# Score products in another order, and one output split moved on VectorE, in a fused attention and expert kernel

## The chip, the cores and the metric

One core of a Trainium2 chip runs the whole program. Its engines work side by side and meet at semaphores: TensorE (PE; its weight loads are listed apart as PEld), VectorE (DVE), ScalarE (ACT), GpSimd (POOL), and SyncE (SP), which issues most transfers. The metric is device time in microseconds (us) of one execution.

## The reference

Everything is float32. x is 32 batches of 256 tokens of width 256, ctx has the same shape, and no key is masked by the input mask.

```
y = x + xattn(layernorm(x), ctx, ctx, Wq, Wk, Wv, Wo, bo, mask)     # 16 heads of 64, causal
out = y + ffn(layernorm(y))

xattn: q = qn@Wq, k = ctx@Wk, v = ctx@Wv          # 256 -> 1024
       dots = q k^T / 8, masked and causal; attn = softmax(dots); (attn v) @ Wo + bo
ffn:   expert = argmax(y_n @ router_w.T + router_b)   # 32 experts
       relu(relu(y_n @ w1[e] + b1[e]) @ w2[e] + b2[e])  for the token's own expert
```

## The kernel before

There are two phases. The first does attention and routing for the 32 batches, one after the other, and writes each token's normalised row into a list of its expert in HBM. The second goes through these lists. The change touches the first phase alone, which takes all but about the last 215 us.

Each engine has its own stream of instructions, written out by hand. A batch b has four **steps**, s = 0 to 3. A step deals with a **quad** of four heads, which are two pairs: i = 0 and i = 1. The two heads of a pair are its two **sides**, and they lie in the two halves of the partitions, so that their two products of 64 rows run on TensorE at the same time. In a step TensorE does, in this order (`iteration` of the tensor block):

- `scores(*ahead, 0, ...)`: the products of queries and keys of pair 0 of the *next* quad, into two banks of psS. Since attention is causal, query rows 0 to 127 need 128 keys (a **narrow** product, 128 columns, it = 0), rows 128 to 255 need 256 (a **wide** one, it = 1). Between narrow and wide stands the wait list `first_ready`.
- `probs_t(b, s, 0)`: the first 4 of the 12 blocks of this quad's probabilities are transposed into psR, by 8 products of 64 columns (line 629).
- `scores(*ahead, 1, ...)`: the same for pair 1, with the wait list `second_ready` between narrow and wide. This is "the second half of a step's scores".
- `probs_t(b, s, 1)`: the other 8 blocks, 16 products.
- `values`: attention output of the quad before, into psO (line 650).
- **pieces**: projections and small products named in `PIECES` ("v1", "q0", "wo", "x2" and so on; "wo" is the product with Wo of the batch before, in step 0), each into one of the three banks of psR.

Float32 products are done in two passes. So the narrow part of a pair is four matrix instructions in the trace (two sides, two passes), and so is the wide part; each has a weight load of its own.

`second_ready` is what `probs_t(b, s, 1)` needs before it writes into psR: the probabilities are normalised (s_pn), the transposes of part 0 have ended (s_pt_half, counted up by the last of them), and the bank 2 of psR was read by whoever reads the last piece in it. In step 1 that is `residual` on VectorE (s_x1, line 943), which reads "wo".

```
def second_ready(b, s, prev, nxt):
    pe.wait_ge(s_pn, 4 * G(b, s))
    pe.wait_ge(s_pt_half, G(b, s))
    for bank, (name, at) in last_in(b, s, prev, nxt).items():
        if bank == 2:
            pe.wait_ge(*emptied(name, at))
```

ScalarE copies psR into PT (line 792), takes the exponentials (`exps`, line 799), and writes the high part of the attention output, OT_hi (`hi_o`, line 807). VectorE masks the scores as they leave psS (`masked`, line 1097, eight instructions a step), multiplies by the reciprocal of the sums (`normalised`, lines 1103 to 1112), writes the low part of the output, OT_lo (`lo_o`, line 1117), and routes tokens in a chain of small instructions (`largest`, `where_largest`, `expert_ids`, `one_hot`, `counted` and so on). `mask_of` (lines 1075 and 1079) makes the mask of the next batch, which the masking of step 3 reads. `lo_o` counts s_o up. TensorE's `values` waits for the s_o of the quad whose output lay in psO before, and "wo" waits for that of its batch's last quad.

Of the kernel before, what the change touches and what calls it, by code (L numbers as in the profile page):

```python
# [16 lines left out]
P = 128  # L17
# [12 lines left out]
def attention_moe(nc, x, ctx, mask, Wq, Wk, Wv, Wo, bo, router_w, router_b, w1, b1, w2, b2, out):  # L30
# [21 lines left out]
    with ExitStack() as es:  # L52
# [190 lines left out]
        def pieces(s, prev, nxt):  # L243

            if s == 0 and not prev:
                return FIRST_0
            return [(name, off) for name, off in PIECES[s] if (off >= 0 or prev) and (off <= 0 or nxt)]
# [5 lines left out]
        def bank_of(s, name, prev, nxt):  # L253
            names = [n for n, off in pieces(s, prev, nxt)]
            return banks(len(names))[names.index(name)]
# [37 lines left out]
        def G(b, s):  # L293

            return QUADS * b + s + 1

        def later(b, s, nxt):

            if s < QUADS:
                return b, s  # L300
            return (b + 1, s - QUADS) if nxt else None
# [199 lines left out]
        def _(pe):  # L501
# [74 lines left out]

            def scores(b, s, i, between=None):
                p = 2 * s + i
                for it, o in ((0, 0), (1, P)):
                    if it and between:  # L580
                        between()
                    for side in range(2):
                        rows = slice(DH * side, DH * side + DH)
                        last = nc.tensor.matmul(psS[:, 2 * i + side, o:o + (it + 1) * P], QT[rows, p, it * P:(it + 1) * P],  # L584
                                                KT[rows, p, 0:(it + 1) * P], start=True, stop=True)
                last.then_inc(s_sc, 1)
# [181 lines left out]
        def dve_read(name, b, bank):  # L768

            src = psR[:, bank, :]  # L770
            if name[0] == "v":
                i = int(name[1])
                nc.vector.wait_ge(s_v_pe, 4 * b + i + 1)
                nc.vector.tensor_copy(V[:, i % 2, 512 * (i // 2):512 * (i // 2) + 512], src[:, :]).then_inc(s_v, 1)  # L774
            elif name == "xt":
                nc.vector.wait_ge(s_xt_hi, b + 1)
                nc.vector.tensor_tensor(flat(XTl), src[:, :], flat(XTh), ALU.subtract).then_inc(s_xt, 1)  # L777
            elif name == "lg":

                nc.vector.wait_ge(s_lg_pe, b + 1)  # L780
                for it in range(TT):
                    last = nc.vector.tensor_tensor(lg[:, it, :], src[:, it * E:(it + 1) * E], rb_b[:], ALU.add)
                last.then_inc(s_lg, 1)
# [128 lines left out]
        def _(dve):  # L912
# [178 lines left out]
            def masked(b, s, i, side):  # L1091

                if side == 0:
                    wait_apart(dve, s_passed, s_sc, 2 * G(b, s) - 1 + i)
                for it, o in ((0, 0), (1, P)):
                    cols, k = slice(o, o + (it + 1) * P), 4 * i + 2 * side + it
                    nc.vector.tensor_tensor_reduce(out=Sm[:, 2 * (s % 2) + i, side, cols], in0=psS[:, 2 * i + side, cols],  # L1097
                                                   in1=MK[:, cols], scale=-SCALE, scalar=3e38, op0=ALU.add, op1=ALU.min,
                                                   accum_out=mneg[:, s % 2, k:k + 1]).then_inc(s_sm, 1)
# [15 lines left out]
            def lo_o(b, s):  # L1115
                dve.wait_ge(s_o_hi, G(b, s))
                nc.vector.tensor_tensor(OTl[:, 2 * s:2 * s + 2, :].rearrange("p a n -> p (a n)"), psO[:, :],  # L1117
                                        OTh[:, 2 * s:2 * s + 2, :].rearrange("p a n -> p (a n)"), ALU.subtract).then_inc(s_o, 1)
# [7 lines left out]
            def iteration(b, prev, prev2, nxt, more):  # L1126
                for s in range(QUADS):
                    ahead = later(b, s + 1, nxt)
                    here = pieces(s, prev, nxt)

                    def read(*names):
                        for name, off in here:
                            if name in names:
                                dve_read(name, b + off, bank_of(s, name, prev, nxt))

                    def mask(i, side):
                        if ahead:
                            masked(*ahead, i, side)

                    def norm(i):  # L1140
                        if ahead:
                            normalised(*ahead, i)

                    def route(on, at, stage):
                        if on:
                            stage(at)

                    if s == 0:
                        mask(0, 0)
                        route(prev2, b - 2, rows_gap)  # L1150
                        mask(0, 1)
                        route(prev2, b - 2, rows_near)
                        mask(1, 0)
                        route(prev2, b - 2, rows_all)
                        mask(1, 1)
                        route(prev2, b - 2, rows_kept)
                        if nxt:
                            sum_ctx(b + 1)
                        route(prev2, b - 2, row_places)
                        if prev:  # L1160
                            lo_o(b - 1, QUADS - 1)
                        route(prev2, b - 2, row_numbers)
                        if more and prev:
                            stats1(b + 2)
                        norm(0)
                        if prev:
                            read("xt")
                        norm(1)
                        route(prev2, b - 2, fills)
                        if not prev:  # L1170
                            read("xt")
                            lo_wo(0)
                            stats1(b + 2)
                        elif more:
                            apply1(b + 2)
                        if nxt:
                            first_key(b + 1)
                    if s == 1:
                        if prev:
                            residual(b - 1, bank_of(0, "wo", prev, nxt))  # L1180
                        mask(0, 0)
                        mask(0, 1)
                        mask(1, 0)
                        mask(1, 1)
                        if prev:
                            stats2(b - 1)
                        norm(0)
                        read("v3")
                        norm(1)
                        lo_o(b, 0)  # L1190
                        if prev:
                            apply2(b - 1)
                        else:
                            lo_wo(1)
                            apply1(b + 2)
                    if s == 2:
                        mask(0, 0)
                        mask(0, 1)
                        mask(1, 0)
                        mask(1, 1)  # L1200
                        norm(0)
                        read("lg")
                        route(prev, b - 1, largest)
                        read("v0")
                        norm(1)
                        route(prev, b - 1, where_largest)
                        if nxt:
                            mask_of(b + 1)
                        route(prev, b - 1, expert_ids)
                        route(prev, b - 1, one_hot)  # L1210
                        lo_o(b, 1)
                    if s == 3:
                        if nxt:
                            halve_of(b + 1)
                        mask(0, 0)
                        mask(0, 1)
                        mask(1, 0)
                        mask(1, 1)
                        norm(0)
                        read("v1")  # L1220
                        route(prev, b - 1, counted)
                        route(prev, b - 1, tiles_over)
                        route(prev, b - 1, tiles_more)
                        norm(1)
                        route(prev, b - 1, tiles_run)
                        route(prev, b - 1, tiles_next)
                        route(prev, b - 1, rows_next)
                        lo_o(b, 2)
# [29 lines left out]
            with dve.Fori(2, B - 2) as b:  # L1258
                iteration(b, True, True, True, True)
# [297 lines left out]
```

## Time and profile before

| | us |
|---|---|
| median of 3 runs | 1508.87 |
| lowest, highest | 1504.34, 1510.36 |
| the profiled execution, whole | 1513.0 |
| its span, from the first to the last instruction | 1511.3 |

The profile's page has the span's busy times by engine, the share of busy time in 40 slices, the chain that ended last, and the costliest groups. The trace was asked further for the order in time of a few stretches of one batch in the middle of the first phase. A batch repeats every 41.2 us there.

### The profile page before, as it was taken

What the parts mean: (1) busy time and instruction counts of PE and PEld (TensorE: products, weight loads), DVE (VectorE), ACT (ScalarE), POOL (GpSimd) and SP (SyncE); (2) the same over time, 40 slices, a digit from 0 to 9 for tenths busy, and PEclk for the clock granted to TensorE, in tenths of its full rate; (3) what the DMA queues carried; (4) which work ended last, traced back from release to release, by engine and by line L of the source; (5) the groups of instructions that cost most, each with busy time, mean ns of one, the idle gap of its engine ahead of it and who ended that gap; (6) DMA issues with size and microseconds to landing.
All of it is one profiled execution on the core that took longest, in us unless ns stands there. A gap on an engine that the chain in (4) does not pass through costs nothing.

```text
span 1511.3 us, 43956 instructions
## 1 busy us (share of the span) xinstructions
PE 1479.1 (98%) x14165; PEld 1283.4 (85%) x14165; DVE 1231.7 (82%) x5088; ACT 1013.6 (67%) x3144; POOL 360.6 (24%) x507
## 2 busy tenths in 40 slices
PE   8999999999999999999999999999999999978997
PEld 7898888888888888888888888888888888865775
DVE  5888888988888888888988888888888988755663
ACT  5767667667677667677666677677677677633663
POOL 3112212211121122222211121122222211112777
PEclk9999999999999999999999999999999999987998
DMA  8643000000000000000000000010000000005650
GB/s 288 128 150 115 29 21 29 29 22 29 29 22 25 25 29 29 27 23 29 29 22 29 28 23 22 29 29 29 23 27 29 29 22 22 15 8 175 212 174 12
DMA packets 70410, 77.85 MB, mean 52 GB/s; under 512 B 11351, under 2 KB 64221, under 8 KB 70369
## 3 DMA queue, kind: packets, MB, share of 16 engines
q1 hardware_dynamic: 62546, 60.37, 13.8%
q0 software_dynamic: 7680, 16.93, 3.1%
q8 instruction: 22, 0.36, 0.1%
q14 instruction: 18, 0.15, 0.0%
q10 hardware_dynamic: 144, 0.03, 0.0%
HBM read 47.61 MB, written 33.88 MB: 54 GB/s over the span
## 4 chain that ended last, share of the span: by engine, by line
PE 93%; DVE 3%; ACT 1%; DMA 1%; POOL 1%; issue 1%; SPq 0%; POOLq 0%; DVEq 0%
PE psR L514 37%; PE psS L584 14%; PE psO L650 12%; PE psR L546 12%; PE psR L629 6%; PE psS L1496 4%; PE psR L505 2%; PE psR L1486 2%; PE psR L556 2%; PE psR L1483 1%; PE psR L1473 1%; PE psO L1473 1%; DVE Sm L1112 0%; ACT Sm L799 0%; DMA lists<-stg,lrow 0%
## 5 line engine op out<-in xcount | busy, mean ns | idle before, releaser
L799 ACT ACTIVATE Sm<-Sm,mneg 128x128 f32<-128x128 f32 (+1 forms) x1024 | 453.5, 456 | 153.6 <-DVE mneg L1097 153.6
L1097 DVE CUSTOM_DVE_ANT_0 Sm<-psS,MK 128x128 f32<-128x128 f32 (+1 forms) x1024 | 303.7, 353 | 4.4 <-PE psS L584 1.9
L792 ACT ACTIVATE PT<-psR 128x512 f32<-128x512 f32 x384 | 201.6, 598 | 134.8 <-PE psR L629 130.9
L584 PE MATMUL psS<-KT,QT 64*128 64x128 f32 (+1 forms) x2048 | 251.5, 356 | 5.0 <-DVE V L774 2.0
L799 ACT ACTIVATION_READ_ACCUMULATOR Sm<-Sm,mneg 128x1 f32 x1024 | 205.5, 201 | 0.0
L650 PE MATMUL psO<-PT,V 128*64 128x256 f32 (+1 forms) x2048 | 196.0, 334 | 0.6 <-DVE OT_lo L1117 0.3
L1112 DVE SCALAR_TENSOR_TENSOR Sm<-Sm,halve,rinv 128x512 f32<-128x512 f32 x256 | 191.4, 748 | 0.0
L584 PEld LDWEIGHTS psS<-KT,QT 64*128 64x128 f32 x2048 | 148.7, 187 | 30.4 <-issue 7.7
L650 PEld LDWEIGHTS psO<-PT,V 128*64 128x64 f32 x2048 | 127.4, 137 | 49.0 <-DVE OT_lo L1117 1.2
L629 PEld LDWEIGHTS psR<-ident,Sm 64*128 64x128 f32 x3072 | 144.5, 139 | 21.1 <-DVE Sm L1112 2.5
L1103 DVE RECIPROCAL rinv<-rsum 128x4 f32<-128x4 f32 x256 | 44.1, 172 | 135.6 <-ACT Sm L799 132.3
L629 PE MATMUL psR<-ident,Sm 64*128 64x64 f32 x3072 | 140.9, 223 | 2.2 <-DVE Sm L1112 2.2
L1109 DVE SCALAR_TENSOR_TENSOR Sm<-Sm,halve,rinv 128x256 f32<-128x256 f32 x256 | 124.1, 485 | 9.1
L756 ACT ACTIVATE KT<-psR 128x512 f32<-128x512 f32 x128 | 75.6, 591 | 55.0 <-PE psR L514 55.0
L514 PE MATMUL psR<-CT_hi,Wk_hi 128*128 128x256 f32 x512 | 108.0, 293 | 1.3 <-ACT PT L792 1.3
L1329 POOL DMA_INDIRECT out<-Y,tok x96 | 94.0, 979 | 49.4 <-issue 27.4
L514 PE MATMUL psR<-XT_hi,Wq_hi 128*128 128x256 f32 x512 | 103.5, 284 | 2.0 <-DVE XT_lo L777 1.3
L514 PE MATMUL psR<-XT_lo,Wq_hi 128*128 128x256 f32 x512 | 103.3, 283 | 0.0
L756 ACT ACTIVATE QT<-psR 128x512 f32<-128x512 f32 x128 | 76.5, 598 | 39.8 <-PE psR L514 39.7
L514 PE MATMUL psR<-CT_lo,Wk_hi 128*128 128x256 f32 x512 | 103.0, 283 | 0.0
L514 PE MATMUL psR<-XT_hi,Wq_lo 128*128 128x256 f32 x512 | 103.0, 283 | 0.0
L514 PE MATMUL psR<-CT_hi,Wk_lo 128*128 128x256 f32 x512 | 102.7, 282 | 0.0
(155 smaller groups left out, 3061.7 us busy)
## 6 DMA issues: line engine op xcount, KB each, us to landing
lists<-pad SPq DMA_DIRECT2D x8, 1560.0 KB, 10.2
XS<-lists SPq DMA_DIRECT2D x48, 260.0 KB, 2.9
x_in<-in_x SPq DMA_DIRECT2D x32, 256.0 KB, 3.0
ctx_in<-in_ctx SPq DMA_DIRECT2D x32, 256.0 KB, 2.6
xr<-in_x SPq DMA_DIRECT2D x32, 256.0 KB, 2.6
W2R<-in_L_ffn_weights SPq DMA_DIRECT2D x1, 2048.0 KB
out<-Y,tok POOLq DMA_INDIRECT x96, 2.4
W2R<-in_L_xattn_Wv SPq DMA_DIRECT2D x2, 512.0 KB, 9.3
```

Of the source, the lines that this page charges most:

```text
L514: last = nc.tensor.matmul(dst, a(k), z(k), start=(n == 0), stop=(n == 3 * len(ks) - 1))
L546: last = nc.tensor.matmul(dst[:, it * D:(it + 1) * D], a[:, t, rows], z[:, t, :], start=(it == 0 and a is OTh and z is Woh and t == 0), st ...
L584: last = nc.tensor.matmul(psS[:, 2 * i + side, o:o + (it + 1) * P], QT[rows, p, it * P:(it + 1) * P], KT[rows, p, 0:(it + 1) * P], start=T ...
L629: last = nc.tensor.transpose(ring[:, o:o + DH], Sm[rows, 2 * (s % 2) + i, side, src:src + P], ident[rows, rows])
L650: last = nc.tensor.matmul(psO[DH * side:DH * side + DH, i * N + t * P:(i + 1) * N], V[:, t, DH * h:DH * h + DH], blocks_of[:, blocks, :, : ...
L756: nc.scalar.activation(T[:, 2 * c:2 * c + 2, :].rearrange("p a n -> p (a n)"), src[:, :], ACT.Copy).then_inc(done, 1)
L792: nc.scalar.activation(PT[:, s % 2, 512 * k:512 * k + 512], psR[:, k, :], ACT.Copy).then_inc(s_pt, 1)
L799: nc.scalar.activation(v, v, ACT.Exp, bias=mneg[:, s % 2, k:k + 1], scale=-1.0, accum_out=rsum[:, s % 2, k:k + 1]).then_inc(s_exp, 1)
L1097: nc.vector.tensor_tensor_reduce(out=Sm[:, 2 * (s % 2) + i, side, cols], in0=psS[:, 2 * i + side, cols], in1=MK[:, cols], scale=-SCALE, sc ...
L1109: nc.vector.scalar_tensor_tensor(out=v, in0=v, scalar=halve[:, 0:1], in1=of[:, :, 0:1].broadcast_to([P, 2, P]), op0=ALU.mult, op1=ALU.mult ...
L1112: nc.vector.scalar_tensor_tensor(out=v, in0=v, scalar=halve[:, 1:2], in1=of[:, :, 1:2].broadcast_to([P, 2, N]), op0=ALU.mult, op1=ALU.mult ...
L1329: nc.gpsimd.indirect_dma_start(out_rows, bass.IndirectOffsetOnAxis(ap=tok[u][:, t:t + 1], axis=0), Y[u][:, t, :], None, bounds_check=last_ ...
```

## The change

In `scores`, the pair i = 1 now does its wide product first and its narrow one second; the waits stay between the two. Pair 0 is as it was. In VectorE's step 2, `lo_o(b, 1)`, which stood last, comes right after `where_largest`; `expert_ids` comes next, and the mask of the next batch after it.

```diff
             def scores(b, s, i, between=None):
                 p = 2 * s + i
-                for it, o in ((0, 0), (1, P)):
-                    if it and between:
+                for n, (it, o) in enumerate((((0, 0), (1, P)), ((1, P), (0, 0)))[i]):
+                    if n and between:
                         between()
...
                         norm(1)
                         route(prev, b - 1, where_largest)
+                        lo_o(b, 1)
+                        route(prev, b - 1, expert_ids)
                         if nxt:
                             mask_of(b + 1)
-                        route(prev, b - 1, expert_ids)
                         route(prev, b - 1, one_hot)
-                        lo_o(b, 1)
```

TensorE's order in step 2 of the loop's batch, second half of the scores (psS takes the scores, KT and QT are keys and queries; L619 belongs to `second_ready`); - is before, + is now:

```order
 L584 MATMUL psS<-KT,QT 128x256
 L629 MATMUL psR<-ident,Sm 128x64 x8
-L584 MATMUL psS<-KT,QT 128x128 x2
+L584 MATMUL psS<-KT,QT 128x256 x2
 L619 REGISTER_ALU [waits first_pair_probsT_in_psum,probs_normalised]
-L584 MATMUL psS<-KT,QT 128x256 [waits q_ready]
-L584 MATMUL psS<-KT,QT 128x256
+L584 MATMUL psS<-KT,QT 128x128 [waits q_ready]
+L584 MATMUL psS<-KT,QT 128x128
 L629 MATMUL psR<-ident,Sm 128x64 x16
 L650 MATMUL psO<-PT,V 64x256 [waits probsT_ready,out_ready]
```

What stood behind the waits and stands ahead of them now is the two products of 256 columns; the two of 128 are behind. The other steps read the same, with other names in the wait.

VectorE's order at the end of step 2 of the loop's batch (OT_lo is the output split, MK the mask, eid and OH the routing, halve the first thing of step 3):

```order
 L973 MAX_INDEX ix<-mx,lg 128x8 [waits route_chain]
 L973 MAX_INDEX ix<-mx,lg 128x8
+L1117 TENSOR_TENSOR OT_lo<-psO,OT_hi 128x512 [waits out_hi]
+L977 REGISTER_ALU
+L978 CAST eid<-ix 128x2 [waits route_chain]
 L1075 SCALAR_TENSOR_TENSOR MK<-maskrow,causal 128x256
 L1079 SCALAR_TENSOR_TENSOR MK<-maskrow,causal 128x128
-L977 REGISTER_ALU
-L978 CAST eid<-ix 128x2 [waits route_chain]
 L981 REGISTER_ALU
 L982 TENSOR_TENSOR OH<-iota_e,eid 128x64 [waits route_chain]
-L1117 TENSOR_TENSOR OT_lo<-psO,OT_hi 128x512 [waits out_hi]
 L1086 TENSOR_SCALAR dead_half<-iota_p,firstk 128x2 [waits mask_chain]
```

The output split passed four instructions, and the cast passed two. The streams of ScalarE, GpSimd and SyncE are the same.

## Rows read from the trace of the kernel before

**Rows 1.** The page: span, and busy time by engine

```profile
span 1511.3 us, 43956 instructions
PE 1479.1 (98%) x14165; PEld 1283.4 (85%) x14165; DVE 1231.7 (82%) x5088; ACT 1013.6 (67%) x3144; POOL 360.6 (24%) x507
```

**Rows 2.** Timeline, step 2: start us, us, engine, line, operation, count, [idle before <-releaser]

```profile
710.85 0.48 PEld L629 LDWEIGHTS psR<-ident,Sm 64*128 64x128 f32 x8
...
711.07 0.41 PE L629 MATMUL psR<-ident,Sm 64*128 64x64 f32 x8
711.25 0.31 PEld L584 LDWEIGHTS psS<-KT,QT 64*128 64x128 f32 x4
711.31 1.11 PE L584 MATMUL psS<-KT,QT 64*128 64x128 f32 x8
...
711.72 0.31 PEld L584 LDWEIGHTS psS<-KT,QT 64*128 64x128 f32 x4 [0.16 <-issue]
...
712.04 0.74 PEld L629 LDWEIGHTS psR<-ident,Sm 64*128 64x128 f32 x16
...
712.25 0.66 PE L629 MATMUL psR<-ident,Sm 64*128 64x64 f32 x16
...
712.85 1.28 PEld L650 LDWEIGHTS psO<-PT,V 128*64 128x64 f32 x16
```

**Rows 3.** Timeline, second half of the scores in step 1

```profile
701.00 0.69 DVE L943 TENSOR_TENSOR stg<-psR,xr 128x512 f32<-128x512 f32 x1
...
701.49 1.06 PE L584 MATMUL psS<-KT,QT 64*128 64x128 f32 x8
...
702.35 0.69 PE L629 MATMUL psR<-ident,Sm 64*128 64x64 f32 x16
```

**Rows 4.** Timeline of TensorE, step 3: second half of the scores

```profile
721.04 0.98 PE L584 MATMUL psS<-KT,QT 64*128 64x128 f32 x8
721.83 0.69 PE L629 MATMUL psR<-ident,Sm 64*128 64x64 f32 x16
```

**Rows 5.** Timeline of weight loads, the same stretch

```profile
722.52 0.20 PEld L650 LDWEIGHTS psO<-PT,V 128*64 128x64 f32 x4 [0.15 <-DVE OT_lo L1117]
```

**Rows 6.** Timeline of TensorE, step 0: second half of the scores

```profile
689.84 0.97 PE L584 MATMUL psS<-KT,QT 64*128 64x128 f32 x8
690.62 0.69 PE L629 MATMUL psR<-ident,Sm 64*128 64x64 f32 x16
```

**Rows 7.** Timeline of VectorE, end of step 2 and start of step 3

```profile
720.92 0.41 DVE L1075 SCALAR_TENSOR_TENSOR MK<-maskrow,causal 128x256 bf16<-128x256 uint8 x1
...
721.45 0.16 DVE L978 CAST eid<-ix 128x2 f32<-128x2 uint32 x1
...
721.79 0.68 DVE L1117 TENSOR_TENSOR OT_lo<-psO,OT_hi 128x512 fp32r<-128x512 f32 x1
722.39 0.22 DVE L1086 TENSOR_SCALAR dead_half<-iota_p,firstk 128x2 f32<-128x2 f32 x1
```

**Rows 8.** Timeline of VectorE: first normalising of step 3, a batch apart; step 0's split

```profile
684.64 0.18 DVE L1103 RECIPROCAL rinv<-rsum 128x4 f32<-128x4 f32 x1 [0.69 <-ACT Sm L799]
...
693.69 0.68 DVE L1117 TENSOR_TENSOR OT_lo<-psO,OT_hi 128x512 fp32r<-128x512 f32 x1
...
725.89 0.18 DVE L1103 RECIPROCAL rinv<-rsum 128x4 f32<-128x4 f32 x1 [0.69 <-ACT Sm L799]
```

**Rows 9.** Timeline of ScalarE in step 3: PT copies

```profile
722.55 1.57 ACT L792 ACTIVATE PT<-psR 128x512 f32<-128x512 f32 x3 [1.80 <-PE psR L629]
```

**Rows 10.** Busy time by stretch: us, then PE, PEld, DVE, ACT, POOL (instructions), clock, DMA

```profile
684.64:694.38 9.74, 9.74 (x100) 8.61 (x99) 9.57 (x48) 6.84 (x21) 0.43 (x2) 1.00 0.00 0
```

**Rows 11.** Timeline of weight loads, start of "wo" in step 0

```profile
694.53 0.78 PEld L546 LDWEIGHTS psR<-Wo_hi,OT_hi 128*128 128x128 f32 x6
```

**Rows 12.** Who waited for whom, 683.9 to 725.15 us (one batch)

```profile
POOL first_masked L392 <- DMA maskrow<-in_mask_BxS_bf: 25.9, 2, 13.0
...
DVE xn L932 <- POOL rstd L387: 0.3, 1, 0.3
```

## The prediction

> **What bounds the kernel now.** The page comes first [rows 1]: TensorE is busy for 1479 of 1511 us, VectorE for 1232, ScalarE for 1014. So TensorE bounds the kernel, but "busy" reaches from a product's start to its modelled end, and short idle times hide under it. So the second view is the timeline of single steps, read by starts.
>
> In step 2 [rows 2] the last of the first 8 transposes ends at 711.48 (711.07 + 0.41). The second half of the scores starts at 711.31. Its first weights are loaded from 711.25. The load of the wide product's weights starts only at 711.72, 0.24 us after the transposes ended, and the row calls 0.16 us of idle time "issue". That is the wait for the transposes' own semaphore, and the instructions behind it. From 711.72 on all runs without a gap: the last wide pass starts at 712.04 (the loads for the transposes go ahead under it) and the transposes at 712.25. So a wide pass takes 0.21, and the load ahead of the first one 0.32 - 0.21 = 0.11. A narrow pass has half the columns: 0.11. The narrow product, with a load of 0.11 from 711.25 and two passes, ends at about 711.58. The array is idle from there to 711.83 (711.72 + 0.11): 0.25 us.
>
> From the first narrow start to the first transpose it takes 0.94 in step 2, 0.86 in step 1 [rows 3], 0.79 in step 3 [rows 4] and 0.78 in step 0 [rows 6]. Without a wait it would be 0.05 (rest of the first load) + 2 x 0.21 + 2 x 0.11 = 0.69. The excess is the idle time: 0.25, 0.17, 0.09 and 0.09.
>
> Third, what TensorE gets from the others. In step 1 the wait list holds VectorE's `residual`, which ends at 701.69 [rows 3], 0.20 after the half started at 701.49. The transposes' semaphore must come at about the same place, since in step 2 they end 0.17 after the half's start. So step 1 is a near tie of TensorE's own transposes and VectorE's chain. In step 0 "wo" starts its loads at 694.53 [rows 11], and the output split that it waits for ends at 694.37 [rows 8]. A wait took 0.24 from end to load in step 2, so this too is nearly a tie. In step 3 the values load at 722.52, with 0.15 of idle time put down to the split [rows 5], which ends at 722.47 [rows 7].
>
> **The change part by part.**
>
> *Wide first, steps 0 and 3.* The wait now stands behind two wide passes, which end 0.05 + 0.43 = 0.48 after the half's start. The restart of the old order comes earlier: the transposes end 0.17 after the start, and the narrow end (0.27) plus an idle time of 0.09 is 0.36. So the wait is wholly covered and the half takes 0.69: a gain of 0.09 in each.
>
> *Step 2.* The restart stays where it is, since the transposes set it: load at 0.41, first pass at 0.52, 0.04 past the end of the wide passes. What is left is two narrow passes, not two wide ones: 0.73 in place of 0.94, a gain of 0.21.
>
> *Step 1.* If `residual` keeps its distance, the restart is at 0.27 + 0.17 = 0.44, covered by 0.48: a gain of 0.17. If TensorE comes earlier against it, the gain within the half rises to 0.21 at most, but the lead is lost to the wait.
>
> TensorE's own sum is 0.09 + 0.17 + 0.21 + 0.09 = 0.56 a batch.
>
> *The output split.* It moves ahead of the mask and the cast, from 721.79 to about 720.92 [rows 7], 0.87 earlier, so that it ends at about 721.60, far ahead of the values. In step 3 it takes 0.69 from the start of the 16 transposes (721.83) to the values' load (722.52) [rows 4, 5]; in step 2, 0.60 (712.25 to 712.85) [rows 2]. So 0.09 us a batch goes. What ScalarE must have done for the split (OT_hi) is not new: it reads the step's values, which ended in the step's first third, and nothing shows an idle time of VectorE there. Behind the split now stand the cast, the mask and the one-hot rows. The mask comes about 0.7 later, ahead of the masking as before, since the work up to line 1086 (722.39) is the same. The mask's semaphore also lets SyncE load the next mask row, 0.7 later; GpSimd waits for that load up to 13.0 us and then for others [rows 12], so it is hidden, until it is 13 us late. The cast and the one-hot instruction no longer stand right behind what they wait for: up to 0.1 us less, in front of ScalarE's exponentials. For these VectorE waits 0.69 anyway [rows 8], so it is counted as nothing.
>
> TensorE alone would then gain 0.56 + 0.09 = 0.65 a batch. **What is late next** decides how much of it stays. VectorE's first normalising in step 3 waits for ScalarE [rows 8], ScalarE's copies wait for the transposes [rows 9], so this point moves with TensorE: 0.09 from its start of step 3. From there VectorE is busy for 9.57 of 9.74 us, up to the split of step 0 [rows 10]; it then goes on to `residual`, behind a norm that GpSimd holds up by 0.3 [rows 12]. This chain gains no more than its anchor's 0.09. TensorE arrives at "wo" 0.09 (step 3) + 0.09 (split) + 0.09 (step 0) = 0.27 earlier, finds the split only 0.09 earlier, and has a margin of 0.16 less the latency of a wait, which I take as 0.04 (bounds: 0, if a wait costs 0.16 from end to load; 0.10, if 0.06). So 0.13 stays at "wo". Then comes step 1's half with its 0.17, or 0.21 if `residual` is late: together 0.30 for these three steps (bounds 0.26 and 0.30), and so most of the part that belongs to the split is lost to this tie. Step 2 adds its 0.21. The chain in step 2 has cover: VectorE waits for ScalarE there for up to microseconds, and both for TensorE.
>
> **The sum.** 0.21 + 0.30 = 0.51 us a batch, over 31 batches with four such halves: 15.8 us. The profiled execution took 1513.0, of which 1511.3 is the span; it would take 1497.2. It lies 4.1 over the median of 1508.87, on which I put the gain, about a hundredth: **1493**.
>
> **The rivals.**
>
> *The chain of VectorE leaves TensorE's gain alone* (faster still). If the waits of "wo" and `residual` have 0.15 us of margin more than I read, all 0.65 stays: 20 us, 1489. For it speaks that the trace names no waiting of TensorE at these two places; against it, how near the two ends lie [rows 3, 8, 11]. Chance 0.2.
>
> *VectorE's chain does not move with TensorE* (no difference). If something other than the transposes sets ScalarE's or VectorE's pace in steps 2 and 3, the tie in step 1 gives back what was gained before it, and 0.17 to 0.21 of one half is left: 5 to 6.5 us, about 1503. Against it: VectorE idles for 0.69 and ScalarE for 1.80 in each step 3 [rows 8, 9]. Chance 0.13.
>
> *The narrow weights are not loaded under the wide passes* (slower). In the old order no scores' load followed a wide pass within the half. If each narrow load waited until the passes ahead were through, the half would take 0.48 + 2 x (0.11 + 0.11) = 0.92 against 0.94, 0.86, 0.79 and 0.78: 0.31 more a batch, less nothing else, 10 us or 1519; it decides from a load exposed by more than 0.14 us a half on average, where the 0.56 is used up. Against it: the transposes' loads start at 710.85 under a wide pass, whose successors start at 711.07, 0.22 later, a pass and no more [rows 2]. Chance 0.06.
> The Trainium skill says in "TensorE: Matmul & The Clock Gate", Part 3 (Packing small matmuls, The mechanism), that a weight load overlaps running products only where its row group differs. By that rule this rival would be the forecast, with a time of 1519. The trace disagrees, since loads for both halves of the rows go ahead under passes on both.
>
> *The change does half of what it says*, because the sequencer needs the covered time for its wait instructions anyway, and the restart slips by 0.1 to 0.2 in each half: a gain of about 0.25 a batch, 8 us, 1501. Chance 0.08.
>
> **How the numbers follow.** The forecast has 0.53. "Same" is within 0.5% of 1508.87, or 7.5 us, about what a measurement of this kernel can tell from no change. Faster: 0.53 + 0.2 + half of the last rival, 0.77. Same: 0.13 + 0.04 = 0.17. Slower: 0.06. The range reaches from 1487 (the faster rival, with 2 us of scatter between runs) to 1503; the slower rival and the far half of the second lie outside.
>
> **What the profile would show.** TensorE in step 2: from the half's first start to the first of the 16 transposes 0.73, in the others 0.69 to 0.81. Step 3: values load 0.60 behind the transposes' start, and no idle time put down to OT_lo. Step 0: "wo" starts its load close behind the end of the split, with an idle time ahead of it. Step 1: the restart follows `residual`. A batch takes 40.7 us, not 41.2 [rows 8]. The forecast is wrong if halves take 0.9 (loads exposed), or if they take 0.7 and the batch is still 41.0 or more (the chain took the gain).

## The result, and the profile after

| | before | changed |
|---|---|---|
| median, us (4 runs each) | 1507.11 | 1489.49 |
| lowest, highest | 1504.34, 1510.36 | 1485.65, 1491.09 |
| ratio, with its 95% interval | | 0.9865 [0.9837, 0.9893] |
| the profiled execution, whole | 1513.0 | 1485.65 |
| its span | 1511.3 | 1483.9 |
| one batch, from the traces | 41.26 | 40.65 |

By the ratio the changed kernel is 1.35% faster. The two medians lie 17.6 us apart, which is 1.2% and inside the interval. The forecast was 1493, with 15.8 us of gain from 0.51 us a batch; a batch gained 0.61.

The page of the changed kernel answers to [rows 1]:

```profile
span 1483.9 us, 43956 instructions
PE 1453.8 (98%) x14165; PEld 1264.7 (85%) x14165; DVE 1224.8 (83%) x5088; ACT 1011.6 (68%) x3144; POOL 358.3 (24%) x507
```

The two spans lie 27.4 us apart, which is more than the change is worth. Two windows of each kernel show why: the first phase up to where its last scores are, and what is behind (first before, then changed; columns as in [rows 10]: us, PE, PEld, DVE, ACT and POOL with instructions, granted clock, DMA share, GB/s).

```profile
16.00:1328.30 1312.30, 1305.39 (x13018) 1151.18 (x13020) 1122.96 (x4719) 918.44 (x2916) 254.36 (x374) 1.00 0.13 39
1328.30:1511.30 183.00, 161.56 (x1065) 120.41 (x1061) 100.61 (x354) 87.73 (x219) 99.03 (x102) 0.89 0.39 120
```

```profile
16.00:1310.00 1294.00, 1287.15 (x13022) 1137.05 (x13023) 1115.38 (x4718) 916.73 (x2916) 252.70 (x374) 1.00 0.14 40
1310.00:1484.00 174.00, 154.05 (x1065) 115.43 (x1061) 101.33 (x354) 87.50 (x219) 98.86 (x102) 0.94 0.41 126
```

The first phase gives 18.3 us (31 batches at 0.61 are 18.9). The other 9 us of the spans lie in the second phase, which has the same 1065 products in both and a mean granted clock of 0.89 against 0.94 (where it falls is shown in the last section). The change does not touch that phase. In the experiments it also varies more than the change is worth, so steps are compared below by the first phase alone, whose clock is 1.00 everywhere.

**Batch by batch.** `residual` (line 943) runs once a batch. Its instructions between 600 and 800 us, first and last start, before and changed; four batches lie between the two:

```profile
L943 DVE TENSOR_TENSOR stg<-psR,xr x5: 692/692/692, 618.5 to 783.5; 128x512 f32<-128x512 f32 x5
```

```profile
L943 DVE TENSOR_TENSOR stg<-psR,xr x5: 692/692/692, 610.6 to 773.2; 128x512 f32<-128x512 f32 x5
```

165.0 / 4 is 41.25, and 162.6 / 4 is 40.65.

**The second half of the scores, step 2**, timeline of TensorE and of its weight loads in the changed kernel, which answers to [rows 2]:

```profile
701.82 0.41 PE L629 MATMUL psR<-ident,Sm 64*128 64x64 f32 x8
702.07 0.91 PE L584 MATMUL psS<-KT,QT 64*128 64x256 f32 x8
702.80 0.66 PE L629 MATMUL psR<-ident,Sm 64*128 64x64 f32 x16
```

```profile
702.01 0.31 PEld L584 LDWEIGHTS psS<-KT,QT 64*128 64x128 f32 x4
702.47 0.31 PEld L584 LDWEIGHTS psS<-KT,QT 64*128 64x128 f32 x4 [0.16 <-issue]
702.69 0.63 PEld L629 LDWEIGHTS psR<-ident,Sm 64*128 64x128 f32 x16
```

The wait is still there, with the same 0.16 us of idle time ahead of the second four loads. The transposes end at 702.23 (701.82 + 0.41), and the load starts 0.24 later, as before. But now two wide passes, until 702.55 (0.48 behind the half's start, as the prediction worked it out), run beside it. From the half's first start to the 16 transposes it takes 0.73 (702.80 - 702.07), where it took 0.94.

The other three, step 3, 0 and 1, which answer to [rows 4], [rows 6] and [rows 3], read 0.71 each (671.65 - 670.94 and so on):

```profile
670.94 0.87 PE L584 MATMUL psS<-KT,QT 64*128 64x256 f32 x8
671.65 0.66 PE L629 MATMUL psR<-ident,Sm 64*128 64x64 f32 x16
```

```profile
680.81 0.87 PE L584 MATMUL psS<-KT,QT 64*128 64x256 f32 x8
681.52 0.66 PE L629 MATMUL psR<-ident,Sm 64*128 64x64 f32 x16
```

```profile
692.42 0.87 PE L584 MATMUL psS<-KT,QT 64*128 64x256 f32 x8
693.13 0.66 PE L629 MATMUL psR<-ident,Sm 64*128 64x64 f32 x16
```

The step that ends with a given half, by the distance from one second half to the next in the traces' own resolution (us). Most tables below are of this kind; step 0's number holds what happens from step 0's half to that of step 1, with "wo" in it.

| from the half of | before | changed | gain |
|---|---|---|---|
| step 3 to step 0 | 10.048 | 9.867 | 0.181 |
| step 0 to step 1 | 11.647 | 11.617 | 0.030 |
| step 1 to step 2 | 9.833 | 9.647 | 0.186 |
| step 2 to step 3 | 9.733 | 9.520 | 0.213 |
| a batch | 41.26 | 40.65 | 0.61 |

**The values of step 3** answer to [rows 5]: the load comes 0.58 behind the transposes (672.23 - 671.65), not 0.69, and no idle time stands ahead of it. The split that it waits for ran at 670.82, ahead of the cast and the mask, where it stood behind them [rows 7]:

```profile
672.23 0.85 PEld L650 LDWEIGHTS psO<-PT,V 128*64 128x64 f32 x12
```

```profile
670.82 0.67 DVE L1117 TENSOR_TENSOR OT_lo<-psO,OT_hi 128x512 fp32r<-128x512 f32 x1
671.41 0.16 DVE L978 CAST eid<-ix 128x2 f32<-128x2 uint32 x1
671.47 0.42 DVE L1075 SCALAR_TENSOR_TENSOR MK<-maskrow,causal 128x256 bf16<-128x256 uint8 x1
```

**"wo" in step 0**, weight loads, which answers to [rows 11], and the split that it waits for, which answers to [rows 8]:

```profile
684.83 0.58 PEld L505 LDWEIGHTS psR<-ident,xn 128*128 128x128 f32 x4
685.48 0.65 PEld L546 LDWEIGHTS psR<-Wo_hi,OT_hi 128*128 128x128 f32 x5
```

```profile
684.68 0.68 DVE L1117 TENSOR_TENSOR OT_lo<-psO,OT_hi 128x512 fp32r<-128x512 f32 x1
```

The small piece ahead of "wo" (line 505) starts its loads 0.65 before those of "wo". Before, these were 0.56 apart (693.97 and 694.53), and so they are in an experiment below that takes this wait away, so 0.56 is how the loads run without a wait. So TensorE now waits here for 0.09, and starts 0.12 behind the end of the split (685.36). This idle time is too short to carry a name in the rows.

### The profile page after: what moved, and what is told of

It reads as the page before. It is cut to its first block, busy times and chain, and to the rows that moved or that the text cites. A ratio compares the mean times of both kernels' runs of the same rounds, so it can differ in the third digit from the quotient of the medians.

```text
span 1483.9 us, 43956 instructions
## 1 busy us (share of the span) xinstructions
PE 1453.8 (98%) x14165; PEld 1264.7 (85%) x14165; DVE 1224.8 (83%) x5088; ACT 1011.6 (68%) x3144; POOL 358.3 (24%) x507
## 4 chain that ended last, share of the span: by engine, by line
PE 93%; DVE 3%; ACT 1%; POOL 1%; issue 1%; DMA 1%; ACTq 0%; DVEq 0%; SPq 0%; POOLq 0%
PE psR L514 37%; PE psS L584 13%; PE psR L546 13%; PE psO L650 12%; PE psR L629 6%; PE psS L1496 3%; PE psR L505 2%; PE psR L1486 2%; PE psR L556 2%; PE psR L1483 1%; PE psR L1473 1%; PE psO L1473 1%; DVE Sm L1112 0%; ACT Sm L799 0%; POOL out L1329 0%
## 5 line engine op out<-in xcount | busy, mean ns | idle before, releaser
L584 PE MATMUL psS<-KT,QT 64*128 64x256 f32 (+1 forms) x2048 | 232.9, 345 | 4.8 <-DVE V L774 2.2
L584 PEld LDWEIGHTS psS<-KT,QT 64*128 64x128 f32 x2048 | 153.4, 187 | 34.0 <-issue 7.2
L629 PEld LDWEIGHTS psR<-ident,Sm 64*128 64x128 f32 x3072 | 134.2, 139 | 14.6 <-DVE Sm L1112 2.7
L629 PE MATMUL psR<-ident,Sm 64*128 64x64 f32 x3072 | 137.8, 222 | 2.4 <-DVE Sm L1112 2.4
L392 POOL CAST first_masked<-maskrow 128x1 f32<-128x1 uint8 x32 | 6.2, 194 | 418.3 <-DMA maskrow<-in_mask_BxS_bf 418.3
```

The costliest lines, as they stand in the source:

```text
L629: last = nc.tensor.transpose(ring[:, o:o + DH], Sm[rows, 2 * (s % 2) + i, side, src:src + P], ident[rows, rows])
```

## The experiments

Every kernel is compared with the kernel before on the same chip. The first four ran on one whose second phase takes some 30 us longer (the kernel before takes 1544.06 there, 13 runs); in the first phase the steps that an edit does not touch agree with the first profiles' to 0.01 us.

### The scores' order alone

```diff
-                for it, o in ((0, 0), (1, P)):
-                    if it and between:
+                for n, (it, o) in enumerate((((0, 0), (1, P)), ((1, P), (0, 0)))[i]):
+                    if n and between:
```

> The order of the scores as changed, the output split left at the end of step 2. Theory A (read from the two traces): in the second halves TensorE gains 0.07, 0.15, 0.21 and 0.07 us in steps 0 to 3 (first start to first transpose), and 0.03 more in steps 0, 1 and 3 at the last transpose. In step 3 the values wait for the output split, which stays 1.43 us after the half's start, so that step gives back its 0.10. A batch takes 40.75 to 40.8 us (before 41.26, changed 40.65): ratio about 0.989 to 0.990. Theory B (the prediction on record): most of what the split gives is lost at wo anyway, so this is as fast as the whole change within 0.05 us a batch, 40.65 to 40.7.

1529.58 against 1544.06: 0.9911 [0.9889, 0.9932]. A batch takes 40.82, a gain of 0.45 of the change's 0.61. Theory A had 40.75 to 40.8 and is close; theory B, with at most 40.7, is refuted. The steps from 3, 0, 1, 2 take 10.049, 11.598, 9.647 and 9.522. The halves are those of the changed kernel. But step 3 gained nothing: what its half saves is given back at its values. Timeline, TensorE and the loads:

```profile
670.96 0.87 PE L584 MATMUL psS<-KT,QT 64*128 64x256 f32 x8
671.67 0.65 PE L629 MATMUL psR<-ident,Sm 64*128 64x64 f32 x16
```

```profile
672.44 0.63 PEld L650 LDWEIGHTS psO<-PT,V 128*64 128x64 f32 x8 [0.25 <-DVE OT_lo L1117]
```

The idle time ahead of the values was 0.15 with the old order [rows 5] and is 0.25 here, with the split as releaser, which in this kernel starts at 671.71 as the last of step 2's instructions. The gain of 0.10 in step 3's half and the growth of this wait by 0.10 cancel.

### The output split alone

```diff
+                        lo_o(b, 1)
+                        route(prev, b - 1, expert_ids)
                         if nxt:
                             mask_of(b + 1)
-                        route(prev, b - 1, expert_ids)
                         route(prev, b - 1, one_hot)
-                        lo_o(b, 1)
```

> The output split moved as changed, the scores in the old order. Theory A: values in step 3 load 0.08 us earlier, but at wo in step 0 TensorE meets VectorE's split with a margin of about 0.05, so a batch gains 0.05: 41.21 us, ratio 0.998 to 1.000. Theory B (parts add up): the whole change's 0.61 less what the scores alone give, 0.10 to 0.15 a batch: 41.12 to 41.16, ratio 0.997. Rival (the split pushes the mask and routing back, which costs): over 41.26.

1541.43 against 1544.06: 0.9977 [0.9957, 0.9997]. A batch takes 41.20, a gain of 0.06, as theory A had it (41.21), and not 0.10 or more. Its reason was another, though: the step with "wo" is as long as before (11.647). Only step 3 changes (9.993 for 10.048): at its values 0.08 is won, and 0.025 of it is lost again in the products that follow.

The two parts alone come to 0.45 + 0.06 = 0.51 us a batch; together they bring 0.61. The split is worth 0.06 by itself and 0.165 once the scores have their new order (40.82 to 40.65), since then it must also keep step 3's own 0.10.

### No product ahead of the wait

From the kernel before: the waits of the second half stand ahead of both its products, so that nothing runs while TensorE waits.

```diff
-                    if it and between:
+                    if it != i and between:
```

> From the kernel before: the waits of the second half stand ahead of both its products, narrow and wide, so that nothing covers them. Theory A (the restart is set by the wait, and what stands behind it is added): second halves, from the restart's first product to the first transpose, have load, two narrow and two wide passes behind the wait. From the last of the first 8 transposes the step 2 half takes 0.21 us more than before (two narrow passes leave the cover), and the others as much, so a batch takes about 4 x 0.21 = 0.84 more, less what ties give back: 41.9 to 42.1 us, ratio 1.014 to 1.021. Rival (the sequencer needs the time for the wait instructions anyway, wherever they stand): no more than 0.3 a batch, 41.3 to 41.6.

1567.86 against 1544.06: 1.0159 [1.0132, 1.0187], 0.77 us a batch slower (42.03), inside theory A's 41.9 to 42.1. Each of the four halves, read from the start of the first 8 transposes to that of the 16, is 0.22 longer; of these 0.89 in sum, 0.77 reach the batch, and where the rest is made up was not followed. Timeline of step 2, TensorE and its loads:

```profile
723.91 0.41 PE L629 MATMUL psR<-ident,Sm 64*128 64x64 f32 x8
724.57 0.93 PE L584 MATMUL psS<-KT,QT 64*128 64x128 f32 x8 [0.25 <-PE psR L629]
725.32 0.66 PE L629 MATMUL psR<-ident,Sm 64*128 64x64 f32 x16
```

```profile
724.56 0.53 PEld L584 LDWEIGHTS psS<-KT,QT 64*128 64x128 f32 x8 [0.38 <-issue]
```

Here the idle time is plain to see, and for once it carries the transposes' name. It makes a series of three with one edit, what stands ahead of the wait. From the start of the first 8 transposes to the start of the 16, step 2: nothing ahead 1.41 (725.32 - 723.91), the narrow product ahead 1.18 (712.25 - 711.07, [rows 2]), the wide one ahead 0.98 (702.80 - 701.82). The work is the same in all three. Each step of it hides about 0.2 us more: the narrow product covers its own two passes of 0.11, and the wide one in its place covers two passes of 0.21.

### "wo" waits for the low part only where it reads it

From the changed kernel: "wo" reads the high part of the output first, in its first 16 products, and the low part behind them. The wait for the low part (s_o) now stands there, and the one ahead of all is for the high part alone.

```diff
-                pe.wait_ge(s_o, G(b, pairs[-1] // 2))
+                pe.wait_ge(s_o_hi, G(b, pairs[-1] // 2))
...
                     for a, z in ((OTh, Woh), (OTh, Wol), (OTl, Woh)):
+                        if it == 0 and a is OTl:
+                            pe.wait_ge(s_o, G(b, pairs[-1] // 2))
```

> The changed kernel, with wo waiting for the high part of the output (out_hi) at its start and for the low part only ahead of the products that read it. Theory A (TensorE loses 0.07 us a batch at wo, since the low part comes late): a batch takes 40.58 us, ratio to the kernel before 0.984 to 0.986, and step 0 from its second half to that of step 1 takes 11.55 in place of 11.62. Rival (TensorE loses nothing at wo; the 0.04 us that step 0 is short of its gain lies elsewhere, in the step's copies or transposes): 40.65, no change to the changed kernel.

1520.24 against 1544.06: 0.9847 [0.9826, 0.9867]. A batch takes 40.55, 0.10 less than the changed kernel, and all of it in the step from 0 to 1 (11.520 for 11.617). Theory A had 40.58 and 11.55; the rival's 40.65 is refuted. Weight loads at "wo", and the split on VectorE:

```profile
683.42 0.58 PEld L505 LDWEIGHTS psR<-ident,xn 128*128 128x128 f32 x4
683.98 1.01 PEld L548 LDWEIGHTS psR<-Wo_hi,OT_hi 128*128 128x128 f32 x8
```

```profile
683.27 0.68 DVE L1119 TENSOR_TENSOR OT_lo<-psO,OT_hi 128x512 fp32r<-128x512 f32 x1
```

"wo" is again 0.56 behind the piece ahead of it. From the half of step 3, which starts at 669.54 here, it starts its loads after 14.44; in the changed kernel after 14.54 (685.48 - 670.94), and before after 14.74 (694.53 - 679.79, where 679.79 is the half's start a batch ahead of [rows 4]). So TensorE reaches "wo" 0.30 earlier than it used to, and the changed kernel keeps 0.20 of it.

### The changed kernel, once more, beside its variants

> The changed kernel itself, on the chip and in the rounds of e6, as the reference for it and for the first four. Batches 40.65 us, attention phase 1293.7 us from first to last scores as in its first trace, whatever the chip; ratio to the kernel before 0.986 to 0.989.

On another chip, where the kernel before takes 1512.67 (7 runs): 1487.13, a ratio of 0.9833 [0.9806, 0.9859], and a batch of 40.65, as expected. The ratio lies below the expected 0.986 to 0.989: the medians are 25.5 us apart here and were 17.6 in the first comparison, while the loop is the same. From the first to the last scores it takes 1291.8 us, not 1293.7. The 31 batches account for no more than 0.2 of this difference, so it lies outside the loop, in the phase's two ends.

### With "wo" as above, and `residual`'s wait for it last

`residual` on VectorE waits for "wo" first, and then for the bias and for two scatters that have long ended. Here the wait for "wo" stands behind these.

```diff
-                dve.wait_ge(s_wo_pe, b + 1)
                 dve.wait_ge(s_bo, 2 * b + 2)
                 if not isinstance(b, int) or b > 0:
                     for it in range(TT):
                         wait_apart(dve, s_passed, s_scat[it], 16 * b)
+                dve.wait_ge(s_wo_pe, b + 1)
```

> e4 and, in VectorE's residual of step 1, the wait for wo's product moved behind the three waits that are satisfied long before. Theory A (residual starts 0.43 us after wo's product ended because its other waits are worked off only then, and VectorE is free 0.08 before): residual starts 0.08 to 0.15 us earlier against step 1's second half, and the batch stays at 40.55, since the wide passes cover that wait. Rival (the chain through GpSimd and the norm sets residual, as the prediction had it): it keeps its distance of 0.49 ahead of the second half's start.

1485.59 against 1512.67: 0.9835 [0.9808, 0.9862], not to be told from the changed kernel by its time. A batch takes 40.55, as without this edit. Timeline of VectorE ahead of `residual` (line 945 here), of this kernel and, as the second, of the changed one:

```profile
649.66 0.42 DVE L1073 TENSOR_REDUCE firstk<-mtmp 128x1 f32<-128x256 f16 x1
650.08 0.69 DVE L945 TENSOR_TENSOR stg<-psR,xr 128x512 f32<-128x512 f32 x1
```

```profile
691.43 0.42 DVE L1071 TENSOR_REDUCE firstk<-mtmp 128x1 f32<-128x256 f16 x1
691.94 0.69 DVE L943 TENSOR_TENSOR stg<-psR,xr 128x512 f32<-128x512 f32 x1
```

In this kernel `residual` follows the instruction ahead of it without a gap, as it nearly does before the change (700.57 + 0.42 to 701.00): VectorE's own work holds it, and no order of waits can bring it forward. In the changed kernel it starts 0.09 behind. There it follows TensorE: it starts 0.45 after the end of "wo", which is at 691.49:

```profile
690.37 1.12 PE L546 MATMUL psR<-Wo_hi,OT_lo 128*128 128x256 f32 x8
```

Theory A is wrong: `residual` starts 0.47 ahead of step 1's second half here, and so it does in the kernel without this edit. It took the gap of 0.09 from the changed kernel, but letting "wo" start earlier had already closed it. The rival has the distance right; its cause, the chain through GpSimd, was not tested apart from VectorE's own work.

### The kernel before, with `residual`'s waits in that order

The same edit of `residual` in the kernel before.

> The kernel before with only the waits of residual reordered. Theory A and the prediction's tie agree here that VectorE's own chain ends 0.01 us before residual starts: no change, batch 41.26, second half of step 1 0.86. If the chain has room after all, that half falls to 0.78, as in steps 0 and 3, and the batch to 41.18.

One execution, 1507.92, beside 1512.67; its batch takes 41.26, as before. The half of step 1 shrinks from 0.86 to 0.85 and nothing else comes of it, as expected. So `residual` did not cost the old kernel more than 0.01 a batch, although it lands in the middle of the half.

## Why the prediction was right in its main reading, and the step that failed

The step that failed is the term for "wo" in step 0. The prediction let VectorE's chain gain no more than 0.09 there, so that 0.13 of TensorE's lead was kept; the chain gained 0.16 and 0.20 was kept. That is 0.07 of the 0.10 us by which a batch gained more than forecast. With this term fell the conclusion that most of the split's worth is lost. The rest comes from step 1's half, 0.19 for 0.17, and from rounding.

| us a batch | forecast | measured | |
|---|---|---|---|
| halves of steps 0, 1, 2, 3 | 0.69, 0.69, 0.73, 0.69 | 0.71, 0.71, 0.73, 0.71 | right |
| gained on the path in the halves | 0.56 | about 0.60 | a term left out |
| the split, at the values of step 3 | 0.09 | 0.08 | right |
| TensorE arrives at "wo" earlier by | 0.27 | 0.30 | |
| VectorE's split is done earlier by | 0.09 | 0.16 | the step that failed |
| of TensorE's lead at "wo" is kept | 0.13 | 0.20 | mis-sized by it |
| step 1, to the half of step 2 | 0.17 | 0.19 | |
| step 2, to the half of step 3 | 0.21 | 0.21 | right |
| a batch | 0.51 | 0.61 | |

**The covered wait.** The main reading was right: the restart after the transposes' semaphore costs the same as before, and what changes is what runs beside it. The series of three above shows this as a cause: what stands ahead of the wait was made both less and more, and the time followed.

**A small term was missing.** The halves come out 0.02 longer than forecast, and yet the gain by steps is 0.10, 0.19, 0.21 and 0.10, 0.04 more in sum than the 0.56. The reason is what "the half" is measured to. The two sides of a pair run beside each other in two halves of the rows. After the old wait the wide passes of the two sides restarted 0.036 apart in steps 0 and 3 (single records of the trace: 721.609 and 721.645), so the last transposes ended later than the first one's start says; in the new order the sides are together again by the time of the 16. The rows show it in the length of the 16 transposes, which is 0.69 in steps 0, 1 and 3 before [rows 3, 4, 6] and 0.66 now. In step 2 the sides restarted only 0.01 apart, the 16 took 0.66 before too [rows 2], and the gain is 0.21 by either count. The excess over the work without a wait was read at the first start of the transposes alone.

**The step that failed, "wo".** The prediction said that VectorE's chain from the first normalising of step 3 to the split of step 0 "gains no more than its anchor's 0.09", on the ground that VectorE is busy there for 9.57 of 9.74 us [rows 10]. The first normalising did gain 0.10 (4.85 behind the half of step 3 before, 4.74 now). But the split came 0.16 earlier, counted from the half of step 3 (684.68 - 670.94 = 13.74, before 693.69 - 679.79 = 13.90). In the 0.17 us that a sum of busy times leaves there is a second anchor: the masking of step 0, which waits for the scores of the first half of that same step. Timeline of VectorE at that place, before and changed, and the scores' order alone as the third:

```profile
689.32 0.68 DVE L1117 TENSOR_TENSOR OT_lo<-psO,OT_hi 128x512 fp32r<-128x512 f32 x1
689.97 0.29 DVE L1097 CUSTOM_DVE_ANT_0 Sm<-psS,MK 128x128 f32<-128x128 f32 x1
```

```profile
680.36 0.68 DVE L1117 TENSOR_TENSOR OT_lo<-psO,OT_hi 128x512 fp32r<-128x512 f32 x1
680.97 0.28 DVE L1097 CUSTOM_DVE_ANT_0 Sm<-psS,MK 128x128 f32<-128x128 f32 x1
```

```profile
680.38 0.68 DVE L1117 TENSOR_TENSOR OT_lo<-psO,OT_hi 128x512 fp32r<-128x512 f32 x1
681.15 0.29 DVE L1097 CUSTOM_DVE_ANT_0 Sm<-psS,MK 128x128 f32<-128x128 f32 x1
```

From the half of step 3 to this masking it took 10.18 before (689.97 - 679.79), takes 10.03 in the changed kernel (680.97 - 670.94) and 10.19 with the scores alone (681.15 - 670.96). The third is the telling one. There VectorE's first normalising came 0.10 earlier as well (675.71 - 670.96 = 4.75), and the instruction ahead of the masking, step 3's own split, stands where it stands in the changed kernel, 9.42 behind the half of step 3 (9.53 before). But TensorE had given its gain back, reached step 0 no earlier (10.05 for 10.05), and the masking waited for it: it starts 0.77 behind that split, where it is 0.61 in the changed kernel, which has no wait there, and 0.65 before. In this kernel and in the one before, the masking starts 0.21 behind the end of that half's scores (single records); in the changed kernel 0.23, since there VectorE's own work is the later of the two. So the chain does not run freely from step 3 to "wo": it is tied to TensorE once more on its way, and goes on from the later of the two. The old kernel's wait there, 0.04 to 0.05, went, and the chain gained this on top of the 0.10.

```profile
675.71 0.18 DVE L1103 RECIPROCAL rinv<-rsum 128x4 f32<-128x4 f32 x1 [0.58 <-ACT Sm L799]
```

At "wo" itself the tie was there, as forecast, and so was its margin: the loads start 0.12 behind the split's end now and 0.16 before, which are the 0.04 of the prediction. The tie took 0.10 of 0.30, and 0.14 of 0.27 was forecast. Moving the wait into "wo" took it away and gave 0.10 a batch back, which shows it as the cause.

**The split.** Its size at the values was right, 0.08 for 0.09; a batch gains 0.06 from it alone. What the prediction concluded, that "most of the part that belongs to the split is lost to this tie", was wrong. It weighed each part against the tie at "wo", but not the parts against each other: without the split moved, the new order's 0.10 in step 3 is lost to the values' wait at once. The old order had idle time in front of two consumers in step 3, the half and the values; filling the first alone only lengthens the second.

**Step 1.** The reading of a near tie was right. `residual` lands 0.21 behind the start of the half (691.94 + 0.69 - 692.42), where it was 0.20 [rows 3], so it moved with TensorE, and in the new order two wide passes, until 0.48, cover it and its restart. That it would move was assumed with the words "if `residual` keeps its distance", and no reason was given. It starts 0.45 behind the end of "wo" in both kernels. In the old one VectorE's own work ended 0.01 ahead of that point, so that two bounds fell together; in the changed one TensorE's is the later by 0.09.

**The mask, 0.7 later.** GpSimd waits 13.5 us for the mask's row where it waited 13.0 [rows 12], and its next one (line 395) takes 9.0 where it took 9.9. Hidden, as forecast.

**The rivals.** That all 0.65 stays came closest in its time, 1489 against the 1489.49 measured, but not in its reason: VectorE's chain does hold TensorE at "wo", and the sum without it is 0.71 (40.55 for 41.26), not 0.65. Its 1489 is luck: TensorE's own terms were taken 0.06 too small, which makes up for most of the 0.10 that the tie costs. That VectorE's chain does not move is refuted by the split's 0.16. That the sequencer needs the covered time is refuted by the restart, which comes 0.24 after the transposes as before. The slower rival, narrow weights exposed behind wide passes, would have made halves of 0.92; they take 0.71 to 0.73.
The Trainium skill, in "TensorE: Matmul & The Clock Gate", Part 3 (Packing small matmuls, The mechanism), has a list that lets a weight load overlap running products only in another row group; by that rule the halves would be 0.92. The changed kernel's trace disagrees once more. The same section says ahead of that list that a load into the background weight buffer is pulled ahead too, which the prediction left out; no row here shows to which buffer a load goes.

**The sum.** 31 x 0.61 is 18.9 us, and the first phase shows 18.3; its two ends were not followed, and they differ by some 2 us between two executions of the changed kernel. The medians differ by 17.6; a batch of 40.65 was measured in both profiled executions of the changed kernel.

**What stays open.** Why 0.025 of the split's 0.08 is lost again within the products behind the values in step 3, when the split alone is moved. Where 0.02 of the 0.30 at "wo" comes from: the halves of steps 3 and 0 and the split make 0.28, and the products of line 514 between the values and "wo" in step 0 take 0.02 less. And the variant with "wo" waiting late is faster by 0.10 us a batch in its trace, some 3 us in all, which its times do not tell from the changed kernel's: 0.9847 and 0.9833 were measured on different chips, and beside the changed kernel only the version with `residual` edited too was run, at 0.9835 against 0.9833.

## What to carry to other kernels

Where an engine must wait in the middle of a sequence whose parts have no order among them, the longest part belongs ahead of the wait: the restart comes at the same time after what it waits for, and what the wait costs the kernel is its length less the work beside it. Before a gain on the bounding engine is added up over a period, look for its next meeting with each other engine, and in the other engine's chain for every place where it waits for the first, however short: a stretch that is busy for 98% can still be tied down in the rest. And measure parts together as well as apart, since a saving ahead of a second wait is worth nothing until that wait moves too.

## What the runs showed of the hardware

The first phase repeats to about 0.01 us a batch in all these runs. The second varies by more than the change is worth. Stretches of 20 us of it, before and changed, at about the same place in the work:

```profile
1350.00:1370.00 20.00, 15.78 (x55) 9.92 (x53) 10.12 (x52) 0.91 (x2) 2.98 (x4) 0.83 0.09 27
1370.00:1390.00 20.00, 17.67 (x82) 11.69 (x81) 9.08 (x32) 8.48 (x21) 4.28 (x5) 0.62 0.79 254
```

```profile
1330.00:1350.00 20.00, 16.29 (x66) 10.16 (x66) 10.21 (x52) 0.91 (x2) 2.98 (x4) 0.91 0.14 38
1350.00:1370.00 20.00, 18.80 (x134) 13.75 (x133) 14.07 (x47) 14.05 (x35) 8.10 (x9) 1.00 0.90 290
```

Between the phases TensorE is busy for about 16 of 20 us, and the granted clock falls from 1.00 to means of 0.83 to 0.91. In the kernel before it is still down in the stretch with the experts' first products (a mean of 0.62, so most of it at 1.2 GHz), where 82 products are done in 20 us; in the changed kernel it is back at 2.4 GHz by then, and 134 are done. On the chip of the first four experiments the whole stretch takes longer still. There the scores-alone kernel has, beside 174.00 us at 0.94 above:

```profile
1312.40:1526.00 213.60, 176.69 (x1067) 128.29 (x1062) 98.22 (x354) 85.98 (x219) 98.94 (x102) 0.85 0.33 103
```

Where a few microseconds are at stake, whole times from different chips or executions say little, and the period of the loop says nearly all.

A wait whose semaphore TensorE itself raised is not free: from the end of the last of the 8 transposes to the next load it is 0.24 us, in the old order and in the new. It is not one price for all waits: at the values of step 3 the load comes 0.05 behind the end of the split [rows 5, 7], and at "wo" 0.12.

A list of waits on VectorE costs time behind the member that is satisfied last. In the kernel with nothing ahead of the wait, VectorE stands idle for `residual`. The first row is TensorE's end of "wo" (713.18), the second `residual`, 0.45 later:

```profile
712.06 1.12 PE L546 MATMUL psR<-Wo_hi,OT_lo 128*128 128x256 f32 x8
713.63 0.69 DVE L943 TENSOR_TENSOR stg<-psR,xr 128x512 f32<-128x512 f32 x1 [0.42 <-PE psR L546]
```

VectorE's sequencer has records of its own in the trace: the wait for "wo" (line 939) goes through 0.04 behind the end of "wo", and the three behind it (lines 25, 27 and 27) and then `residual` follow about 0.1 apart each. The copy of V (line 774) has no such list behind its wait for TensorE, and starts within 0.04 of the last product's end, 718.68 in the kernel before:

```profile
718.06 0.62 PE L514 MATMUL psR<-Wv_hi,CT_lo 128*128 128x512 f32 x2
718.71 0.69 DVE L774 COPY V<-psR 128x512 f32<-128x512 f32 x1 [0.18 <-PE psR L514]
```

Putting the wait for "wo" last changed nothing in this case, since VectorE's own work came later still. What it saves where VectorE is idle, no run shows.
